# An ending written out by hand for an adaLN attention and FP4 feed-forward kernel: early sums of the output projection, rounding on VectorE, idle PSUM banks, two stores

## The reference

```python
# x: (32, 256, 128); c: (32, 128); 16 heads of 64; w_gate, w_up: (352, 128); w_down: (128, 352)
mod = (silu(c) @ wmod).reshape(32, 6, 1, 128)
sa, ca, ga, sb, cb, gb = (mod[:, n] for n in range(6))      # ga, gb: |.| at least 0.25, sign kept
h = layernorm(x) * (1 + ca) + sa
# attention: q, k, v from h; p = exp(s - rowmax), causal; out = (p @ v) / (sum(p) + 1e-8)
x = x + ga * (attention(h) @ Wo + bo)
h = layernorm(x) * (1 + cb) + sb
# fp4_linear: both operands quantized in blocks of 16 along the last dimension, scale = max|.| / 6
g = silu(fp4_linear(h, w_gate)) * fp4_linear(h, w_up)
x = x + gb * fp4_linear(g, w_down)
```

## Time and profile before

| what | us |
|---|---|
| median of 3 runs (lowest to highest) | 1317.78 (1317.76 to 1317.88) |
| the profiled execution, its own time | 1317.02 |
| its span, from first to last instruction | 1314.9 |
| mean granted TensorE clock, as a share of full speed | 0.988 |

### The profile page before, as it was taken

One profiled execution on the slowest core, in us unless ns is written; L12 is line 12 of the kernel. 1 busy time (PEld: TensorE's weight loads), 2 busy tenths in 40 slices (PEclk: granted clock), 3 DMA queues, 4 the chain that ended last, 5 costly groups with the idle time before them and its releaser, 6 DMA issues.

```text
span 1314.9 us, 34208 instructions
## 1 busy us (share of the span) xinstructions
PE 1268.4 (96%) x10194; PEld 1031.1 (78%) x10194; DVE 1086.3 (83%) x2557; ACT 838.2 (64%) x2892; POOL 848.3 (65%) x1595
## 2 busy tenths in 40 slices
PE   6899999999999999999999999999999999999984
PEld 4678888878888878878878888878888878888863
DVE  6678888888888888888889888888888888988765
ACT  5766666766666766666766666676666676666640
POOL 5656666676666676666676666676666666666654
PEclk9999999999999999999999999999999999999995
DMA  3000000000000000000000000000000000000000
GB/s 109 17 15 23 18 10 22 18 22 22 16 10 22 18 22 22 16 16 16 18 22 22 16 20 12 18 22 22 19 19 10 22 18 22 20 17 6 19 19 10
DMA packets 38920, 26.53 MB, mean 20 GB/s; under 512 B 2896, under 2 KB 34128, under 8 KB 38896
## 3 DMA queue, kind: packets, MB, share of 16 engines
q1 hardware_dynamic: 38480, 25.96, 6.8%
q10 hardware_dynamic: 416, 0.26, 0.1%
HBM read 21.94 MB, written 4.28 MB: 20 GB/s over the span
## 4 chain that ended last, share of the span: by engine, by line
PE 92%; DVE 3%; POOL 2%; ACT 1%; issue 1%; DMA 0%; DVEq 0%; POOLq 0%
PE ps_m L1029 27%; PE ps_s L1128 18%; PE ps_m L1003 16%; PE ps_o L1158 14%; PE ps_m L1081 9%; PE ps_s L1138 5%; PE ps_m L1105 4%; ACT probs L659 0%; DVE neg_max L858 0%; DVE probs_t L793 0%; DVE xn L782 0%; POOL probs L451 0%; POOL rstd L495 0%; DVE qy L62 0%; DVE h_r L874 0%
## 5 line engine op out<-in xcount | busy, mean ns | idle before, releaser
L659 ACT ACTIVATE probs<-ps_s,neg_max 128x128 f32<-128x128 f32 (+1 forms) x1024 | 424.2, 429 | 391.9 <-PE ps_s L1138 391.9
L451 POOL TENSOR_SCALAR probs<-probs,r_den 128x256 f32<-128x256 f32 (+1 forms) x768 | 346.4, 466 | 0.0
L858 DVE TENSOR_REDUCE neg_max<-ps_s 128x4 f32<-128x1024 f32 x256 | 304.0, 1219 | 7.0 <-PE ps_s L1128 6.9
L1128 PE MATMUL ps_s<-qk 64*128 64x256 f32 x2048 | 258.5, 391 | 0.6 <-ACT qk L617 0.6
L793 DVE COPY probs_t<-ps_m 128x512 f32<-128x512 f32 x256 | 176.6, 690 | 78.4 <-PE ps_m L1003 74.3
L1003 PE MATMUL ps_m<-ident,probs 128*128 128x128 f32 x1536 | 230.8, 273 | 2.8 <-DVE probs_t L793 1.6
L1128 PEld LDWEIGHTS ps_s<-qk 64*128 64x128 f32 x2048 | 185.1, 186 | 47.8 <-issue 12.4
L449 POOL TENSOR_TENSOR probs<-probs,r_den 128x128 f32<-128x128 f32 x256 | 102.6, 401 | 185.6 <-DVE r_den L869 166.7
L659 ACT ACTIVATION_READ_ACCUMULATOR probs<-ps_s,neg_max 128x1 f32 x1024 | 217.3, 212 | 0.0
L73 POOL TENSOR_TENSOR qy<-qy,qm 128x352 f32<-128x352 f32 (+1 forms) x96 | 83.0, 865 | 183.6 <-DVE qm L66 181.2
L1158 PE MATMUL ps_o<-probs_t,v 128*64 128x256 f32 (+1 forms) x2048 | 195.4, 333 | 1.5 <-ACT o_t L649 1.5
(11 more groups left out here) (110 smaller groups left out, 1800.8 us busy)
## 6 DMA issues: line engine op xcount, KB each, us to landing
mod_a<-mod_rows SPq DMA_DIRECT2D x32, 256.0 KB, 3.3
x_res<-L_attn_x SPq DMA_DIRECT2D x32, 128.0 KB, 2.1
out<-y_out SPq DMA_DIRECT2D x32, 128.0 KB, 1.8
x_in<-L_attn_x SPq DMA_DIRECT2D x31, 128.0 KB, 2.1
mod_b<-mod_rows SPq DMA_DIRECT2D x32, 64.0 KB, 2.8
wkv<-L_attn_Wkv SPq DMA_DIRECT2D x3, 256.0 KB, 5.8
wo<-L_attn_Wo SPq DMA_DIRECT2D x1, 512.0 KB, 5.5
wkv<-L_attn_Wkv SPq DMA_DIRECT2D x2, 128.0 KB, 3.1
```

Of the source, the lines that this page charges most:

```text
L451: ins = nc.gpsimd.tensor_scalar(cols, cols, r_den[:, u % 4, s:s + 1], 1.0, ALU.mult, ALU.mult)
L659: ins = nc.scalar.activation(probs[:, u % 4, h, t * P:(1 + 2 * t) * P], ps_s[:, 2 * (u % 2) + h, t * N:t * N + (1 + t) * P], ACT.Exp, bias ...
L858: nc.vector.tensor_reduce(neg_max[:, u % 4, :], ps_s[:, 2 * (u % 2):2 * (u % 2) + 2, :].rearrange("p b (t j) -> p (b t) j", t=2), AX.X, AL ...
L1128: mm = nc.tensor.matmul(ps_s[:, 2 * (u % 2) + h, t * N:(t + 1) * N], qk[rows, u % 4, 0, t * P:(t + 1) * P], qk[rows, u % 4, 1, :], start=( ...
```

## The change

The body runs up to batch 31's attention pass only. What passes 32 and 33 did stands after the loop in an order of its own, on each engine.

- **PE.** `shared_step` takes its destination as an argument. In the ending the idle banks of the scores and of the values are used too: transposes of batch 31 go to `ps_s`, pair 3's values to `ps_s[3]` in place of `ps_o`. The projection's two sums are begun before all pairs are there: units 0 to 3 of tile 0 after the first transposes, the rest after pair 3's values. The gates and ups of a batch have a bank each.
- **ACT** copies pair 2's values right away, and writes the high half of the quantized input (`xq_r[0]`), which VectorE did.
- **DVE** does the two modulating instructions of batch 31, the rounding of its feed-forward input and the rounding of its second hidden tile, all three of which GpSimd did. Its own work on batch 30's second hidden tile stands behind the input of batch 31.
- **POOL** keeps the inverse deviation and the rounding of three hidden tiles; the copy of batch 31's sum (`x1_keep`) falls away, `x1` is read instead.
- **SP.** Batch 31's gate row has a buffer of its own (`mod_last`) and is loaded after the loop; the last batch is stored from `x_in`, one transfer for each tile.

```diff
-            for i in range(last, B + 2):
+            for i in range(last, B):
                 body(i)
...
             iterations(sp, body, B - 2)
-            sp.wait_ge(stored, 16 * B)
+            sp.dma_start(mod_last[:, :], mod_rows[LAST, 4].partition_broadcast(P)).then_inc(mod_last_loaded, 16)
+            sp.wait_ge(down_scaled, 2 * FORE)
+            sp.dma_start(mod_b[:, :], mod_rows[FORE, 4].partition_broadcast(P)).then_inc(mod_b_loaded, 16)
+            sp.wait_ge(y_ready, 2 * LAST)
+            sp.dma_start(out_v[FORE], y_out[:, :, :]).then_inc(stored, 16)
+            for t in range(2):
+                sp.wait_ge(y_ready, 2 * LAST + t + 1)
+                sp.dma_start(out_v[LAST][:, t, :], x_in[:, t, :]).then_inc(stored, 16)
+            sp.wait_ge(stored, 16 * (B + 1))
...
             iterations(pool, body)
+            normalize_unit(LAST, UNITS - 1)
...
+            round_hidden_half(FORE, 0)
+            rstd(LAST, ln2_pool, x1_steps, X1_STEPS * B, mv2, var2, rstd2)
+            round_hidden_half(FORE, 1)
+            round_hidden_half(LAST, 0)
...
+            last_out_copy(2, ps_o[:, :])
+            last_transposed(0)
+            act.wait_ge(xqt_full, LAST)
+            nc.scalar.copy(xq_r[0][:, :], ps_m[0][:, 0:N]).then_inc(xqt_high, 1)
+            last_transposed(1)
+            last_tanh(FORE, 0, ps_s[:, 0, 0:I])
+            last_out_copy(3, ps_s[:, 3, :])
+            last_tanh(FORE, 1, ps_s[:, 2, 0:I])
+            last_hidden_copy(FORE, 0, ps_o[:, 0:IP])
...
+            last_gated(FORE, 0, ps_s[:, 0, 0:I])
+            last_hidden(FORE, 0, ps_s[:, 1, 0:I])
+            last_hidden_scales(FORE, 0)
+            last_attended(0)
+            last_attended(1)
+            dve.wait_ge(x1_steps, X1_STEPS * LAST + 2)
+            layer_norm_stats(x1, stats2, mv2, x1_steps, X1_STEPS * LAST + 2)
+            last_gated(FORE, 1, ps_s[:, 2, 0:I])
+            last_hidden(FORE, 1, ps_m[0][:, 0:I])
...
+            nc.vector.tensor_tensor(h2a_v, xn2_v, both_tiles(mod_a[:, 2, :]), ALU.mult).then_inc(h2a_ready, 1)
+            dve.wait_ge(h2a_ready, B)
+            nc.vector.tensor_tensor(h2_v, h2a_v, both_tiles(mod_a[:, 3, :]), ALU.add).then_inc(h2_ready, 1)
...
+            quantize_round(nc.vector, Steps(dve, xq_round, ROUND_STEPS, LAST), xq, 2 * P // BLOCK, scale[0], qy[0], qm[0])
+            last_down(FORE, 0, ps_m[2][:, 0:P], mod_b[:, :], (mod_b_loaded, 16 * LAST), x1_keep, y_out)
+            dve.wait_ge(xqt_high, 2)
+            nc.vector.tensor_tensor(xq_r[1][:, :], ps_m[1][:, 0:N], xq_r[0][:, :], ALU.subtract).then_inc(xqt_ready, 2)
+            last_hidden_scales(FORE, 1)
+            last_gated(LAST, 0, ps_s[:, 0, 0:I])
+            last_hidden(LAST, 0, ps_s[:, 1, 0:I])
+            last_hidden_scales(LAST, 0)
+            last_gated(LAST, 1, ps_s[:, 2, 0:I])
+            last_hidden(LAST, 1, ps_m[0][:, 0:I])
+            last_hidden_scales(LAST, 1)
+            dve.wait_ge(hqt_full, 2 * LAST)
+            quantize_round(nc.vector, Steps(dve, hq_round[1], ROUND_STEPS, LAST), hq[:, 1, :], I // BLOCK, scale[2], qy[2], qm[2])
+            last_down(FORE, 1, ps_o[:, 0:P], mod_b[:, :], (mod_b_loaded, 16 * LAST), x1_keep, y_out)
+            for k in range(2):
+                last_down(LAST, k, ps_s[:, k, 0:P], mod_last[:, :], (mod_last_loaded, 16), x1, x_in)
...
+            last_values(2, ps_o)
+            shared_step("t", LAST, 9, ps_s[:, 0, :])
...
+            last_attended(0, range(0, 4))
...
+            shared_step("xqt", FORE, 0, ps_m[0])
+            shared_step("t", LAST, 10, ps_s[:, 1, :])
+            shared_step("t", LAST, 11, ps_s[:, 2, :])
...
+            shared_step("gate", FORE, 0, ps_s[:, 0, :])
...
+            shared_step("up", FORE, 0, ps_s[:, 1, :])
+            last_values(3, ps_s[:, 3, :])
...
+            last_attended(1, range(0, 6))
+            last_attended(0, range(4, 6))
+            pe.wait_ge(ot_ready, PAIRS * B)
+            last_attended(0, range(6, 8))
+            last_attended(1, range(6, 8))
+            shared_step("gate", FORE, 1, ps_s[:, 2, :])
+            shared_step("up", FORE, 1, ps_m[0])
+            shared_step("hqt", FORE, 0, ps_o)
...
+            shared_step("down", FORE, 0, ps_m[2][:, 0:P])
+            shared_step("xqt", LAST, 0, ps_m[1])
...
+            shared_step("hqt", FORE, 1, ps_s[:, 3, :])
+            shared_step("down", FORE, 1, ps_o)
+            shared_step("hqt", LAST, 0, ps_m[1])
+            pe.wait_ge(gated, 2 * LAST + 1)
+            shared_step("down", LAST, 0, ps_s[:, 0, :])
+            shared_step("hqt", LAST, 1, ps_s[:, 3, :])
+            pe.wait_ge(h_ready, 2 * LAST + 1)
+            shared_step("down", LAST, 1, ps_s[:, 1, :])
```

More of the change, by code:

```diff
@@ L145, in adaln_block @@
         mod_b = sb("mod_b", [P, P])
+        mod_last = sb("mod_last", [P, P])
         stats1 = sb("stats1", [P, 2, 6])
@@ L372, in adaln_block @@
         POOL_SETUP = 7
+        LAST, FORE = B - 1, B - 2
+        BANK_LEFT = {}
+        for _, (kind, b, part, bank, _) in sorted(shared_steps(LAST).items()):
+            BANK_LEFT[bank] = (kind, b, part)
         block = ctx.enter_context(nc.Block())
@@ L1030, in matmul_parts, with shared_step @@
                 return mm
-            def shared_step(kind, b, k, bank):
+            def shared_step(kind, b, k, dst):
                 if kind == "t":
@@ L1118, in at_place @@
                             pe.wait_ge(*bank_read(*before))
-                        shared_step(kind, b, k, bank)
+                        shared_step(kind, b, k, ps_m[bank])
                 def scores(u):
@@ L1229, in _, with last_values @@
             for place in ((2, 8), (3, 1), (3, 6)):
-                shared_step(*shared[place][0:4])
+                kind, b, k, bank, _ = shared[place]
+                shared_step(kind, b, k, ps_m[bank])
             iterations(pe, body)
+            def last_values(pair, dst):
+                for g in range(3):
+                    pe.wait_ge(pt_ready[g], PAIRS * LAST + pair + 1)
+                for k in range(2):
+                    for n, (keys, q0) in enumerate(((0, 0), (1, P))):
+                        for h in range(2):
+                            col = (2 * (2 * pair + k) + h) * DH
+                            chunk = 3 * (2 * k + h)
+                            mm = nc.tensor.matmul(dst[h * DH:(h + 1) * DH, k * N + q0:(k + 1) * N], v[:, keys, col:col + DH],
+                                                  probs_t[:, chunk + 2 * n:chunk + 2 + n, :],
+                                                  start=(n == 0), stop=(n == 1), skip_group_check=True)
+                mm.then_inc(o_full, 1)
@@ new lines, in last_attended @@
+            def last_attended(k, units):
+                for u in units:
+                    mm = nc.tensor.matmul(ps_m[1 + k][:, 0:P], o_t[:, u, k * P:(k + 1) * P], wo[:, u, :],
+                                          start=(u == 0), stop=(u == UNITS - 1))
+                if u == UNITS - 1:
+                    mm.then_inc(wo_full, 1)
+            pe.wait_ge(v_ready, 4 * B)
+            pe.wait_ge(ot_ready, PAIRS * LAST + 2)
+            last_values(2, ps_o)
+            shared_step("t", LAST, 9, ps_s[:, 0, :])
```

119 lines of the change are left out of this document (107 added, 12 removed).

## The result

| | kernel before | changed kernel |
|---|---|---|
| median of 4 runs (lowest to highest), us | 1317.77 (1317.66 to 1317.88) | 1305.72 (1304.05 to 1307.45) |
| profiled execution: its time, its span, us | 1317.02, 1314.9 | 1304.05, 1302.4 |
| mean granted clock | 0.988 | 0.991 |

The ratio is 0.9909, with a 95% interval of 0.9892 to 0.9926: 12.05 us less, against a forecast of 11.6 (1306.2). The spans of the profiled executions differ by 12.5, their own times by 12.97: an execution's own time lies 1.65 over its span now, and lay 2.12 over it.

What follows compares the result with a forecast made beforehand. TensorE paces the kernel up to batch 31; the ending is bound by a chain of short dependent steps. Terms -0.75 - 5.45 - 3.8 - 1.6 = -11.6 us took 1317.78 to 1306.2, range 1304.2 to 1308.9.

Steps and rivals of the forecast that it cites:

- Stage 1: Ending up to the first gate: gate starts at 1268.95 instead of 1269.69, 0.75 us gained.
- Stage 2: From first gate to `x1`: PE runs without a hole, `x1` ends at 1275.95 against 1282.16, 5.45 us in the sum.
- the cover of the last add: End of the projection: the last add into `x1` takes 0.57 us with POOL at work.
- Stage 3: From `x1` to xq rounded: xq's transposes start at 1283.15 instead of 1293.13, 3.8 us gained in this stage.
- Stage 4: From xq's transposes to the last `y`: ends at 1301.1, taking 18.0 us instead of 19.6.
- Stage 5: The final store: 2.15 us from issue to span end, with nothing gained from half the bytes.
- the four banks remove the waits: Stage 4, gate, tanh and up lie under batch 30's second chain without bank waits; no separate size given.
- The collision: VectorE's moved work and GpSimd's rounding delay each other: +2.4 and up to 2.1 us, 1308.6 to 1310.7; chance 0.10.
- the room that was forecast: Stage 4, GpSimd is idle by 1.2 us at VectorE's last moved rounding.
- TensorE's clock: Rival: full clock comes back in Stage 4, speeding hqt and down, -1.8 us to 1304.4; chance 0.06.

Runs made afterwards that it cites:

- two-banks kernel: Changed kernel with each batch's second gate and up reusing the first's banks, and pair 3's values in `ps_o`: ending 37.89 us, ratio 0.9893.
- chain-first kernel: Changed kernel with scales and quotient of batch 30's second hidden tile ahead of batch 31's normalization: ending 41.37 us against 37.9, ratio 0.9925.
- same again: Changed kernel profiled and timed once more with no edit: ending 37.85 us, ratio 0.9908.
- one store: Changed kernel with the last batch stored in one transfer of both tiles: ending 37.90 us, ratio 0.9909.
- filled gaps: Changed kernel with unread matmuls in TensorE's wait ahead of batch 31's xq transposes and in six later waits: ending 37.71 us, ratio 0.9914.
- five parts undone: Changed kernel without early sums, early pair 2 copy, batch 30's moved second chain, and VectorE's input (with modulation) and second-hidden-tile rounding: ending 44.04 us, ratio 0.9954.

## Why the prediction was right, point by point

- **The ending is a chain and nothing ahead of it moves: right.** 12.36 of 12.5 us lie in the ending.
- **Stage 1, first gate at 1268.95:** 1268.8 by the chain, of which 0.14 is the earlier start. The early sum fitted into the gap (eight instructions, 1.06 us from 1265.99), the high half took 0.37 on ScalarE (I had 0.4).
- **Stage 2, `x1` at 1275.95:** 1275.53. The term that was mis-sized is gate and up, "1.5 (0.73 each)": the pair takes 0.95 of the chain. In the timeline six such matmuls in a row show 1.20 and three show 0.73, and the group behind starts before their shown end. The step that failed is the cover of the last add: it took 0.78 against GpSimd, not 0.57. Of the 0.77 by which pair 3's values came earlier than forecast, 0.42 are left at `x1`. The clock stayed at 1.00, as argued. The chain's view of gate, up and values:

```profile
1268.80 0.95 PE ps_s L1175 x6
1269.75 1.45 PE ps_s L1388 x16
```

- **Stage 3, xq's transposes at 1283.15:** 1282.51; the stage took 6.98, forecast 7.2. VectorE's roundings took 0.42 to 0.43 (0.44). Undone alone: +1.6.
- **Stage 4, last sum at 1301.1:** 1300.18. The first chain against GpSimd took 2.81 (1287.63 to 1290.44), not 3.0, and the second 2.85 (1291.66 to 1294.51). Rounding took 1.65, as priced; undone alone it costs 1.2. "Down" of tile 0 ended 0.4 behind it, as priced too.
- **Stage 5: right within the span.** 2.2 us from the last sum to the span's end in both kernels. The prediction also kept 2.1 from the span to the execution's own time; that part shrank to 1.65. At most 0.25 of this is told by the two stores, the rest stays open.
- **Sum.** The end of the last sum came 0.92 earlier than forecast: 0.42 of it by `x1`, 0.22 in stage 3 and 0.28 in stage 4, where the two chains against GpSimd give 0.34. So the mechanism held, and each stage gave somewhat more than its term. The profiled executions' own times differ by 12.97: 12.36 in the ending, 0.14 ahead of it, and about 0.5 outside the span. That the medians come nearer to the forecast (12.05 against 11.6) is partly luck: by their times, two of the changed kernel's four runs (1306.67 and 1307.45) had the long start, and none of the kernel before's. In the next comparison the same two kernels' medians differ by 10.55, with the ending unchanged.
- **Where it credited the wrong part.** I let "the four banks remove the waits" in stage 4. The two-banks kernel shows that given this order the banks are worth nothing. Whether they were needed to write the order was not tried. And batch 30's second chain, which I only booked as moved from stage 3 to stage 4, is the edit whose undoing costs most in the runs (3.5). Of that 1.4 is the order; 2.0 come up only because the chain put wholly ahead of the normalization lets GpSimd's rounding run against VectorE.
- **Rivals.** The collision was real in kind and absent where it would have counted: 0.44 and 0.48 of added time on the two chains (0.30 and 0.85 for 0.18 and 0.53 in the first), none on the moved roundings. The last of these began 1.2 us behind GpSimd's end (1293.37 and 1294.54), the room that was forecast. TensorE's clock did not come back in stage 4 of this profile. In six others it did, the same again and one store among them, and their endings were 37.85 and 37.90. The rival's 1.8 was the price of the last hqt and "down" of both tiles, and these ran at half all the same: in the same again the clock was 0.67 in the window 1291, 1.00 from 1292 to 1295, and half from 1296 on, and the last "down" took 1.62. The filled gaps, at 1.00 to the end, show what it gives there (0.91 for "down"). The Trainium skill ("SBUF — State Buffer", "Who interferes with whom") says that a VectorE instruction with two SBUF inputs and a GpSimd instruction that reads SBUF exclude each other. The chain-first kernel agrees: 2.12 for 0.61, and the pair ends 0.1 behind GpSimd's second instruction.

What stays open is how the last 6.2 us divide between order, banks and clock; the kernel with five parts undone only gives their sum.

## What to carry to other kernels

When the steady state is full but the drain isn't, write the drain as its own schedule: there the length of the dependent chain counts, not how busy an engine is. Start each sum with the operands that are there, copy what others wait for before what only its own chain needs, and give the chain's elementwise steps to the faster engine once it has time. Where VectorE and GpSimd slow each other down, the order decides twice: a step moved earlier can set the other engine going just where the chain is (2.0 us here). Measure such an edit on the stretch that it changes; executions that differ by 3 us in their start hide an edit of 1 us from the medians.

## What was not expected of the hardware

- TensorE's clock falls in the start-up of some executions and not of others of the same program (1.00 against 0.50 in the window 22 to 24), which gave 1.6 of the 2.9 us by which one profile ran longer than another. The other 1.25 arose in 16 matmuls that took 3.47 us in place of 2.22 while the clock's row showed 1.00.
- Fillers meant to hold the clock up can meet it already down: 5.07 us for 18 matmuls of 512 columns in place of 4.05, and the real work waits behind them.
- Six matmuls of 352 columns in two groups take 0.95 us of the chain, where a group of three by itself shows 0.73.
